# Row maxima of attention scores: from a bounce through DRAM to four extra matrix products per step

## What is computed

```python
qr, kr, vr = (to_regions(q), to_regions(k), to_regions(v))      # 49 regions of 64 positions per image
logits = jnp.einsum('brc,bsc->brs', qr.mean(2), kr.mean(2))
_, idx = jax.lax.top_k(logits, 4)                               # every region attends to 4 regions
kg = take(kr, idx); vg = take(vr, idx)                          # 256 keys per region
scores = jnp.einsum('brqhd,brkhd->brhqk', qh, kh) * scale       # 8 heads of 8 channels
attn = jax.nn.softmax(scores, axis=-1)
out = jnp.einsum('brhqk,brkhd->brqhd', attn, vh) @ wo + bo
x = x + out
x = x + (gelu(layernorm(x) @ w1 + bm1) @ w2 + bm2)
```

## Time and profile before

| | us |
|---|---|
| runs of the kernel before | 5547.73 median of 3 (5535.24 to 5552.67) |
| profiled execution, span from first to last instruction | 5568.0 |
| PE busy, matmuls | 4677.0 (84%) |
| PEld busy, weight loads | 3217.0 (58%) |
| DVE busy | 3447.6 (62%) |
| ACT busy | 3285.4 (59%) |
| POOL busy | 2747.0 (49%) |

### The profile page before, as it was taken

The page is one execution under the profiler, slowest core; times in us unless marked ns, Lnnn a source line. Parts: engine busy times, 40 slices in busy tenths (PEclk is TensorE's granted clock), DMA queues, the critical chain, the costliest instruction groups (busy, mean ns, idle before and its releaser), DMA issues.

```text
span 5568.0 us, 230234 instructions
## 1 busy us (share of the span) xinstructions
PE 4677.0 (84%) x68754; PEld 3217.0 (58%) x68754; DVE 3447.6 (62%) x7969; ACT 3285.4 (59%) x6282; POOL 2747.0 (49%) x9656
## 2 busy tenths in 40 slices
PE   2388888888889888888888888888888888888888
PEld 1265565656556565565656656565565656556564
DVE  2266666666666666666666666666566666667665
ACT  1156556565665656556565665656556565665656
POOL 1245455454544545445454554545455454554553
PEclk8589999998998999889989999989899999989999
DMA  1333343333333333333333423333343333323311
GB/s 53 102 98 92 83 109 76 100 77 96 102 77 98 84 95 91 82 103 80 94 83 91 111 72 103 81 96 92 79 109 79 96 81 102 100 75 102 84 40 33
DMA packets 627124, 487.33 MB, mean 88 GB/s; under 512 B 483792, under 2 KB 613968, under 8 KB 615536
## 3 DMA queue, kind: packets, MB, share of 16 engines
q10 hardware_dynamic: 335360, 205.62, 16.4%
q1 hardware_dynamic: 290416, 265.73, 16.2%
HBM read 262.38 MB, written 208.73 MB: 85 GB/s over the span
## 4 chain that ended last, share of the span: by engine, by line
PE 45%; DMA 18%; issue 10%; SPq 7%; ACT 7%; DVE 5%; DVEq 3%; POOL 2%; ACTq 2%; POOLq 1%
DMA max_d<-tr 11%; PE ps L988 9%; PE ps L1002 7%; PE ps L1019 7%; PE ps L881 4%; DMA qm<-qk_d 3%; PE ps L938 3%; DMA xin<-in_x 3%; DVEq L223 2%; DVE mx L724 2%; SPq L327 2%; PE ps L949 2%; PE ps L901 2%; ACT hid L813 2%; PE ps L974 2%
## 5 line engine op out<-in xcount | busy, mean ns | idle before, releaser
L724 DVE TENSOR_REDUCE mx<-ps 128x4 f32<-128x1024 f32 x1568 | 1921.7, 1226 | 1702.3 <-PE ps L988 1354.0
L832 ACT ACTIVATE pt<-ps 128x512 f32<-128x512 f32 x3136 | 1694.3, 592 | 869.2 <-PE ps L1002 814.4
L506 POOL COPY vg<-vs 64x64 f32 x6272 | 1526.5, 243 | 782.0 <-POOL kg L490 576.7
L988 PE MATMUL ps<-kg,qm 96*128 96x256 f32 x6272 | 1336.2, 338 | 386.6 <-DVE mx L724 127.3
L490 POOL CAST kg<-ks 96x128 fp32r x3136 | 851.0, 297 | 1511.6 <-PE ps L1002 1156.6
L988 PEld LDWEIGHTS ps<-kg,qm 96*128 96x128 f32 x6272 | 946.8, 202 | 1053.6 <-issue 889.5
L1002 PE MATMUL ps<-qm,kg 97*128 97x256 f32 x6272 | 1119.8, 301 | 178.8 <-ACT pt L832 102.3
L1019 PE MATMUL ps<-pt,vg 128*32 128x64 f32 x50176 | 1091.4, 231 | 0.0
L1002 PEld LDWEIGHTS ps<-qm,kg 97*128 97x128 f32 x6272 | 926.2, 203 | 252.2 <-ACT pt L832 164.8
L1019 PEld LDWEIGHTS ps<-pt,vg 128*32 128x32 f32 x50176 | 826.1, 115 | 224.2 <-issue 34.8
L643 DVE CAST kg<-ks 96x128 fp32r x3136 | 625.6, 241 | 126.2 <-issue 123.5
(11 more groups left out here) (109 smaller groups left out, 3866.7 us busy)
## 6 DMA issues: line engine op xcount, KB each, us to landing
qk_d<-stg SPq DMA_DIRECT2D x224, 448.0 KB
qm<-qk_d ACTq DMA_DIRECT2D x1792, 42.0 KB
ks<-qk_d ACTq DMA_DIRECT2D x96, 784.0 KB, 6.2
vs<-v_d ACTq DMA_DIRECT2D x64, 784.0 KB, 6.7
xin<-in_x SPq DMA_DIRECT2D x119, 224.0 KB
xi_d<-xi SPq DMA_DIRECT2D x112, 224.0 KB
qk_d<-stg SPq DMA_DIRECT2D x112, 224.0 KB
max_d<-tr SPq DMA_DIRECT2D x1568, 2.0 KB
```

What stands on the lines that cost most here:

```text
L506: j = pool.tensor_copy(dst.rearrange("p j (e x) -> p j e x", e=2)[:, :, :, 0:HD], vs[place(m)[0]][rows, bass.ds(region, 1), :].rearrange(" ...
L724: v.tensor_reduce(mx[h % 2][:].rearrange("p (g j e) -> p g j e", g=2, j=2)[:, :, :, 0], ps[:, 0:2, :].rearrange("p g (j k) -> p g j k", j= ...
L832: act.activation(pt[m % 2][:, c], ps[:, 2 + c, :], ACT.Exp, scale=float(HD) ** -0.5).then_inc(S["pt_ready"], 1)
L988: i = pe.matmul(ps[:, g, 256 * j:256 * j + 256], qm[c % 2][0:NP3, t, g, 2 * j:2 * j + 2, :].rearrange("p h t -> p (h t)"), kg[slot][0:NP3, ...
```

## The change

The maxima no longer leave the core. The transpose, both DMAs, the DRAM buffer and the semaphores around them are gone. `mx` is a tile of 128 x 2 x 2. Per step, `turned` issues four more products that add minus the maximum in PSUM: one column of `mx`, repeated 128 times, is the stationary operand, and minus the identity, repeated twice, is the moving one (256 columns). They write the two halves of a bank at once. `turned` is regrouped: bank 2 + g now holds head group g instead of key block b. The lags shrink: `turned` handles region h-1 instead of h-3, `attended` h-2 instead of h-4. ACT copies `um` of region h-3 (before: h-4), and does so ahead of the exponentials instead of behind them. The loads move from ACT's list and queue to the head of SP's step, the query loads two per step at t = 2, 3, 4, 5.

```diff
-ST_LAG = 3
-PV_LAG = 4
+ST_LAG = 1
+PV_LAG = 2
+UM_LAG = 3
...
-            if t in (3, 4, 5) and live((c + 1) * NW, kind):
+            if t in (2, 3, 4, 5) and live((c + 1) * NW, kind):
-                if t == 3 and not (kind == "lead" and c < 1):
+                if t == 2 and not (kind == "lead" and c < 1):
                     eng.wait_ge(S["st_full"], (p * STEPS + c * NW) * 2)
...
 SP, step:
-                if live(m, kind):
-                    sp.wait_ge(hopped[m % 2], (p * R + m // 2 + 1) * 16)
-                    sp.dma_start(qm[m // NW % 2][NP3:NP3 + 1, m % NW]..., max_d[m % RING]...).then_inc(row_ready[m % RING], 16)
-                if live(h, kind):
-                    sp.wait_ge(S["tr_ready"], T + 1)
-                    sp.dma_start(max_d[h % RING]..., tr[h % 2][0:128:8, :]).then_inc(hopped[h % 2], 16)
+                loads(sp, p, h, kind)
...
 DVE, step:
                     v.wait_ge(S["sm_full"], T + 1)
-                    if live(h - 2, kind):
-                        v.wait_ge(hopped[h % 2], (p * R + (h - 2) // 2 + 1) * 16)
-                    v.tensor_reduce(mx[h % 2][:].rearrange("p (g j e) -> p g j e", g=2, j=2)[:, :, :, 0],
+                    v.tensor_reduce(mx[h % 2][:],
                                     ps[:, 0:2, :].rearrange("p g (j k) -> p g j k", j=2), AX.X, ALU.max).then_inc(S["mx_ready"], 1)
                 if live(h + AHEAD, kind):
                     keys(p, h + AHEAD, kind)
-                if live(h, kind):
-                    v.wait_ge(S["mx_ready"], T + 1)
-                    v.transpose(tr[h % 2][:], mx[h % 2][:]).then_inc(S["tr_ready"], 1)
...
 ACT, step:
+                m = h - UM_LAG
+                if live(m, kind) and group_end(m):
+                    u = 2 if m % NW % 2 else 1
+                    act.wait_ge(S["u_full"], T - UM_LAG + 1)
+                    act.activation(merged(m, u), ps[:, 4, 0:RT * u], ACT.Copy).then_inc(S["um_ready"], 1)
                 m = h - ST_LAG
                 if live(m, kind):
...
-                m = h - PV_LAG
-                if live(m, kind) and group_end(m):
-                    u = 2 if m % NW % 2 else 1
-                    act.wait_ge(S["u_full"], T - PV_LAG + 1)
-                    act.activation(merged(m, u), ps[:, 4, 0:RT * u], ACT.Copy).then_inc(S["um_ready"], 1)
-                loads(act, p, h, kind)
                 if kind != "lead":
                     hidden(p, h)
...
 PE, turned:
-                pe.wait_ge(row_ready[slot], (p * 14 + c + 1) * 16)
-                for b in range(2):
+                pe.wait_ge(S["mx_ready"], T + 1)
+                for g in range(NG):
...
-                    for g in range(NG):
-                        i = pe.matmul(ps[:, 2 + b, 256 * g:256 * g + 256],
-                                      kg[slot][0:NP3 + 1, g, 2 * b:2 * b + 2, :]..., qm[c % 2][0:NP3 + 1, t, g]..., start=True, stop=True)
+                    for b in range(2):
+                        pe.matmul(ps[:, 2 + g, 256 * b:256 * b + 256],
+                                  kg[slot][0:NP3, g, 2 * b:2 * b + 2, :]..., qm[c % 2][0:NP3, t, g]..., start=b == 0, stop=False)
+                    for j in range(2):
+                        i = pe.matmul(ps[:, 2 + g, :].rearrange("p (b j n) -> p b j n", b=2, j=2)[:, :, j, :],
+                                      mx[m % 2][:, g, j:j + 1].broadcast_to([128, 128]),
+                                      minus_r[:].unsqueeze(1).broadcast_to([128, 2, 128]), start=False, stop=j == 1)
                     i.then_inc(S["st_full"], 1)
```

More of the change, by code:

```diff
@@ L146, in build @@
         vg = [sb(f"vg{i}", [128, 2 * VG + 8]) for i in range(RING)]
-        mx = [sb(f"mx{i}", [128, 32]) for i in range(2)]
-        tr = [sb(f"tr{i}", [128, 32]) for i in range(2)]
+        mx = [sb(f"mx{i}", [128, NG, 2], F32R) for i in range(2)]
         pt = [sb(f"pt{i}", [128, 2, 512]) for i in range(2)]
@@ L251, in loads @@
             t, c = h % NW, h // NW
-            if t in (3, 4, 5) and live((c + 1) * NW, kind):
-                if t == 3 and not (kind == "lead" and c < 1):
+            if t in (2, 3, 4, 5) and live((c + 1) * NW, kind):
+                if t == 2 and not (kind == "lead" and c < 1):
                     eng.wait_ge(S["st_full"], (p * STEPS + c * NW) * 2)
                     settled(eng)
-                queries(eng, p + (c + 1) // 14, (c + 1) % 14, [(g, h) for g in range(NG) for h in range(HG)][(t - 3) * 3:(t - 2) * 3])
+                queries(eng, p + (c + 1) // 14, (c + 1) % 14, [(g, h) for g in range(NG) for h in range(HG)][(t - 2) * 2:(t - 1) * 2])
             if kind == "loop":
@@ L412, in before @@
                 route(0, 0)
+                first_loads(sp)
             sp.wait_ge(S["zeroed"], 1)
@@ L829, in step @@
                         act.wait_ge(S["u_full"], T - ST_LAG - 2 + 1)
-                    for c in range(2):
-                        act.wait_ge(S["st_full"], (T - ST_LAG) * 2 + c + 1)
-                        act.activation(pt[m % 2][:, c], ps[:, 2 + c, :], ACT.Exp, scale=float(HD) ** -0.5).then_inc(S["pt_ready"], 1)
-                m = h - PV_LAG
-                if live(m, kind) and group_end(m):
-                    u = 2 if m % NW % 2 else 1
-                    act.wait_ge(S["u_full"], T - PV_LAG + 1)
-                    act.activation(merged(m, u), ps[:, 4, 0:RT * u], ACT.Copy).then_inc(S["um_ready"], 1)
-                loads(act, p, h, kind)
+                    for g in range(NG):
+                        act.wait_ge(S["st_full"], (T - ST_LAG) * 2 + g + 1)
+                        act.activation(pt[m % 2][:, g], ps[:, 2 + g, :], ACT.Exp, scale=float(HD) ** -0.5).then_inc(S["pt_ready"], 1)
                 if kind != "lead":
@@ L996, in turned @@
                 c, t, slot = m // NW, m % NW, m % RING
-                pe.wait_ge(row_ready[slot], (p * 14 + c + 1) * 16)
-                for b in range(2):
+                pe.wait_ge(S["mx_ready"], T + 1)
+                for g in range(NG):
                     if not (isinstance(T, int) and T == 0):
-                        pe.wait_ge(S["pt_ready"], (T - 1) * 2 + b + 1)
-                    for g in range(NG):
-                        i = pe.matmul(ps[:, 2 + b, 256 * g:256 * g + 256],
-                                      kg[slot][0:NP3 + 1, g, 2 * b:2 * b + 2, :].rearrange("p k t -> p (k t)"),
-                                      qm[c % 2][0:NP3 + 1, t, g].rearrange("p h t -> p (h t)"), start=True, stop=True)
+                        pe.wait_ge(S["pt_ready"], (T - 1) * 2 + g + 1)
+                    for b in range(2):
+                        pe.matmul(ps[:, 2 + g, 256 * b:256 * b + 256],
+                                  kg[slot][0:NP3, g, 2 * b:2 * b + 2, :].rearrange("p k t -> p (k t)"),
+                                  qm[c % 2][0:NP3, t, g].rearrange("p h t -> p (h t)"), start=b == 0, stop=False)
+                    for j in range(2):
+                        i = pe.matmul(ps[:, 2 + g, :].rearrange("p (b j n) -> p b j n", b=2, j=2)[:, :, j, :],
+                                      mx[m % 2][:, g, j:j + 1].broadcast_to([128, 128]),
+                                      minus_r[:].unsqueeze(1).broadcast_to([128, 2, 128]), start=False, stop=j == 1)
                     i.then_inc(S["st_full"], 1)
@@ L1017, in attended @@
                     for j in range(4):
-                        w, n = c * VG + VC * j + HD * e, 128 * j + RT * e
+                        w, n = c * VG + VC * j + HD * e, 256 * c + 128 * (j % 2) + RT * e
                         i = pe.matmul(ps[32 * j:32 * j + 32, 4, RT * u:RT * u + RT], vg[slot][:, w:w + 32],
-                                      pt[m % 2][:, c, n:n + RT], start=c + e == 0, stop=c + e == 2)
+                                      pt[m % 2][:, j // 2, n:n + RT], start=c + e == 0, stop=c + e == 2)
                 i.then_inc(S["u_full"], 1)
```

21 lines of the change are left out of this document (3 added, 18 removed).

## The result

The changed kernel takes 5803.89 us (median of 4 runs, 5799.87 to 5810.93), the kernel before 5544.25 us beside it: a ratio of 1.0472, with a 95% interval of 1.0445 to 1.0499. It is slower, by 260 us; forecast were 5700 us, in a range of 5,400 to 5,880. The profiled execution of the changed kernel spans 5798.1 us.

A forecast was written before the change was run, and what follows sets the result against it. It took the exchange with DVE to set the pace in light steps and PE in full ones. 323 + 266 − 476 + 40 = +153 us on 5547.7 gave 5700 us, range 5,400 to 5,880.

The forecast's parts named there:

- (c): Waits for the maxima's DRAM bounce and late query loads go away: 476 us gained, between 178 and 525.
- (a): Four added products on PE, 0.48 us per step, paid in full in 37 of 98 steps: 323 us.
- (b): `attended` waits for ACT's `um` copy behind gelus and table load after each strip's MLP, plus smaller places: 266 us.
- (d): PE's clock drops more often at the new stall: a third of 112 strips lose 1.7 us; +40 taken.
- 7 (centring) pay about 0.2 each: Seven centring steps per pair were to pay about 0.2 us each for the added products, 1.4 us.
- the smaller places: Waits for `um` in the layer-norm step, 0.65 us, and with the MLP's norm, 0.2 us: 64 us together.
- the factor 0.86: Share of DVE's 346.7 us wait for the bounce said to reach PE: 298 us.
- second rival: Denser PE work holds the clock at 2.4 GHz, making the kernel faster: 5407 us; chance 0.13.
- The copy in time: PE reaches `attended` no earlier than ACT the `um` copy, so that stall vanishes: 5346 us; chance 0.18.
- One queue: x, xf and query loads stand behind 784 KB loads on SP's queue: about 5,900 us; chance 0.11.
- Split output: Added products writing two separate runs of 128 columns cost double, 323 us more: about 6,020 us; chance 0.03.
- Gain and cost cancel: Removed waits at 525, `um` stall at 202 and no clock loss give 5548 us; chance 0.08.

The follow-up runs named there:

- e6: Kernel before without the maxima's way through DRAM, all loads moved to SP and query loads at t = 2 to 5: 5093.12 us.
- e7: Changed kernel with the old lags, the `um` copy behind the exponentials and ahead of the gelus, four `mx` buffers: 5473.48 us.
- e1: Changed kernel without its four added products per step, maxima taken but not subtracted: 5426.49 us.
- e2: Changed kernel with the `um` copy, of region h-2, moved behind the exponentials and ahead of the gelus: 5414.56 us.
- e9: Changed kernel with `turned` computed three times over in the step behind a strip's MLP step, the last counting: 5614.91 us.
- e5: Kernel before without the transpose, both DMAs of the maxima and their waits; lags and loads as before: 5279.42 us.
- e3: Changed kernel with all loads back in ACT's list and queue, behind the exponentials: 5864.65 us.
- e4: Changed kernel with each added product writing one run of 256 columns instead of two of 128: 5797.49 us.
- e10: Changed kernel with `turned` computed twice over in the step behind a strip's MLP step: 5617.30 us.

## Why the prediction was right, and where it was off

The sign and the mechanism were right: two new costs on PE outweigh the bounce. The measured 5804 us lie 104 us above the forecast, inside its own range of 5612 to 5849. The runs form a chain from the kernel before to the changed one, in which each link holds a few edits that belong together, and the terms of the sum can be laid beside them:

| term | forecast | measured | from |
|---|---|---|---|
| (c) bounce and late loads removed | −476 | −453 | before to e6 |
| (a) added products | +323 | +380 | e6 to e7 |
| (b) `um` behind the gelus, with (d) the clock | +306 | +330 | e7 to changed |
| sum | +153 | +257 | the kernel before beside e6 to changed |

The last link, +330, is the +389 of the order on ACT less the 59 us that the shorter lags gain. Two of the three terms are near their forecast because errors inside them cancel; that is luck, and said below.

**(a) The price was right, the sorting of the steps wrong.** Products cost 1.04 − 0.57 = 0.47 us per step in the trace where 0.48 was forecast. Counted from one `scores` to the next (medians over 14 pairs), the changed kernel against e1 has 35 of 98 steps that pay over 0.42 us (forecast: 37) and another 23 that pay 0.2 to 0.42, 0.35 on average. That nearly all of the price hides in a light step holds for steps with no side work at all: the 17 of them in a pair pay 0.06 us in the median. The term that failed is "7 (centring) pay about 0.2 each, 1.4 us; the others about 1 us together". The seven centring steps pay 0.37 each, and steps with one other short piece of side work mostly 0.3 to 0.5. PE was their bound already, as the 2.24 of 2.24 us above show.

**(b) and (d): the right place, a near sum by luck.** The prediction had `attended` wait about 2 us per strip for `um`, behind the table load; 106 such waits of 2.3 us are in the trace. It gave them 202 us, the smaller places 64, and the clock 40. The smaller places hardly came: their waits are 0.15 to 0.17 us where 0.65 and 0.2 were forecast, some 10 us in all. The order on ACT costs about 200 us as waiting and 189 as clock (e2 and e9). So the estimate for the clock is the other term that failed: "If a third of 112 strips lose 1.7 us". The 1.7 us were right, 189 / 112 = 1.7; the third was wrong, since nearly every strip loses them (105 stretches at the lower clock, 25 before).

**(c) Right as a sum, by two errors.** The removed bounce gave 267 us, not 372: the factor 0.86 came from a single pair of stretches, and over the whole span only 267 of 347 + 74 us came back, 0.63. The loads gave 186 us, not 104: the waits of the earlier trace rows named only what PE waited at, and those waits make 77 of the 186 us. The prediction also read the earlier trace rows too freely, with "the rest is almost all PE". By engine the chain had PE at under half:

```profile
PE 45%; DMA 18%; issue 10%; SPq 7%; ACT 7%; DVE 5%; DVEq 3%; POOL 2%; ACTq 2%; POOLq 1%
```

**The clock of the whole.** The mean rose from 0.909 to 0.941, though the forecast had it cost 40 us; the gain came with the removal of the bounce (0.932 in e5) and the late loads (0.964 in e6), and part of it was given back at the stall (0.977 in e7, 0.941 in the changed kernel). Counted as the prediction counts, the time at the lower level fell from 1,013 to 2 × 0.059 × 5798 = 684 us, at half speed up to 165 us of gain. So the sign that the prediction named for its second rival was partly seen; the rival was right in its direction, and smaller than either of the new costs.

**The other rivals.** The copy in time: no, PE is there 2.3 us too early. One queue: no, e3; and ACT's waits for x fell from 199.2 us before to 81.5, with 81.8 in e3. Split output: no, e4. Gain and cost cancel: no.

**A version that beats both.** e2 keeps the subtraction by products and all else of the change, and moves only the copy: 5414.56 us, 2.3% under the kernel before and 6.7% under the changed one. With it the change is a gain: −453 for the bounce and the loads, +380 for the products, and −59 for the shorter lags.

What stays open: how much of the 186 us of the loads is the clock and how much the waits and ACT's list; and why only 0.63 of the waiting for the bounce came back. That the fill of e9 costs time of its own is not seen: e10, with half of it, takes the same time within 2 us.

## What to carry to other kernels

When lags are shortened, follow each wait to the instruction that now stands ahead of its releaser on that engine; here five lines in another order decided between 2.3% faster and 4.7% slower. Cover for added work has to be read from every kind of step, by PE's busy time over the step's length, not from the one with the most room. And a stall of PE is priced with the steps behind it: their durations at the lower clock belong to its cost.

## What was not expected of the hardware

Redundant work made the kernel faster: 112 times 1.9 us of products whose results are thrown away (the wait fell from 2.31 to 0.42 us) took 189 us off (e9), since PE's clock stayed at 2.4 GHz where it had fallen to 0.53 of it behind 2.31 us of idling; with half of that work, and 1.38 us still idle, it stayed up as well (e10). By the Trainium skill (TensorE: Matmul & The Clock Gate, Part 1) the throttled state is the default and activity releases it; the trace agrees, at 0.53 with PE busy just behind the stall and 0.99 in the next stretch:

```profile
2557.90:2560.80 2.90, 2.90 (x46) 1.82 (x45) 1.49 (x3) 1.08 (x2) 0.85 (x4) 0.99 0.00 0
```
